# Building an adjacency matrix from edge one-hots on TensorE: source index split into tile and place, one wide moving one-hot per edge tile

## The chip, the cores and the metric

One core of one Trainium2 chip runs the whole program. The metric is the device time of one launch in microseconds (us). The kernel before takes 3161.21 us, the median of 3 runs (3160.83 to 3163.68).

## The reference, cut to what matters

The program is a two-block graph network: 1250 nodes with 768 features, 40,000 edges. Both blocks need the graph only as dense matrices over (source, destination): a count matrix (how many edges go from s to d) and a weighted one (the sum of the weights of these edges, with the identity added).

```python
def _scatter_add(tgt, idx, src, axis=0):
    return tgt.at[idx].add(src)
...
src = jax.random.randint(jax.random.fold_in(_gk, 2), (40000,), 0, 1250, jnp.int32)
dst = jax.random.randint(jax.random.fold_in(_gk, 3), (40000,), 0, 1250, jnp.int32)
_o = jnp.argsort(dst, stable=True)
src = src[_o]
dst = dst[_o]
edge_weight = jax.random.uniform(jax.random.fold_in(_gk, 12), (40000,), jnp.float32, 0.0, 0.999998)
```

The edges are sorted by destination. The change lies wholly in the stage that builds these two matrices, the first of the program; the attention, the mixers and the expert layers that follow it are the same in both kernels.

## The kernel before, in words

**Data.** An edge tile is 128 edges, one per partition; there are 313 of them, held as columns of `src_c`, `dst_c` and the weights. Eight edge tiles (`SPREAD`) form a block, 40 blocks (`NB`) form the stage. As the edges are sorted, the 1024 edges of a block touch a short window of destinations, `WIN` = 38 wide, whose start `base[b]` comes from the data. The weight is split into three bf16 parts (`w_c[0..2]`) that add up to the fp32 value. A slower branch (`Else`) stands for edge lists where the window does not hold; here `flag` is 0 and the first branch runs.

**One block, before.** VectorE (DVE) makes the destination one-hot of all eight tiles in one instruction of 304 (8 x 38) elements (L1645) and its three products with the weight parts, 304 elements each (L1651); that is `destinations`. It sets the window for the next block (L1664, 38 elements, `next_block`), and then makes seven source one-hots of 1250 elements, one per edge tile (L1660, `sources`). The eighth source one-hot is made by ScalarE (ACT) in two passes (L1304, L1306). TensorE (PE) does ten matmuls per edge tile (L890): the stationary operand is a slice of 125 columns of the source one-hot, the moving one is 152 columns (4 kinds x 38) of the destination one-hot; it accumulates over the eight tiles in PSUM, in half of the array `ps` (`par` is the half, block number modulo 2). ACT copies the 1520 columns to SBUF (`stage_block`, L1316 and L1318). GpSimd (POOL) adds them into the big matrices `CT` and `WA` at the window's place (`unstage`): it sums the three weight parts (L749, L752), adds the counts (L750) and the weights (L756), each 125 x 380.

**What orders it.** Each engine runs its instructions in program order; counters (semaphores) join them. `src_hot`, `src_hot_act` and `dst_hot` tell PE that one-hots are there, `tiles_done` tells DVE and ACT that PE is through with a tile and its buffers are free (eight source buffers, `RING`), `staged` and `unstaged` join ACT and POOL. Ahead of the stage DVE runs a chain in which each instruction waits for the one before it (`chain`, L1598 to L1637): the edges are converted, turned and split there. Behind the stage DVE's next work is the first layer norm (L1689 to L1701), and PE's next is the transposes of its output (L931).

```python
            def sources(col, tile0):

                for u in range(SPREAD - 1):
                    dve.wait_ge(ev("tiles_done"), tile0 + (u + 1 - RING + CREDIT))
                    dve.tensor_scalar(oh_src[:, u % RING, :], iota_src, src_c[:, bass.ds(col + u, 1)], None,
                                      ALU.is_equal).then_inc(ev("src_hot"), 1)
```

A scalar operand such as `src_c[:, bass.ds(col + u, 1)]` is called a pointer scalar below: one value per partition, read from SBUF, at an address that a register gives.

Of the kernel before, what the change touches and what calls it, by code (L numbers as in the profile page):

```python
# [46 lines left out]
RING = 8  # L47
# [168 lines left out]
def build(nc: bass.Bass, A, out):  # L216
    packets, pieces, last, packet_at = make_plan()

    with ExitStack() as ctx:
# [61 lines left out]
        def ecut(n):  # L281
# [4 lines left out]
        iota_src = ecut(625).bitcast(FP16)  # L286
        src_c = ecut(ECOLS)
        dst_c = ecut(ECOLS)
        w_c = [ecut(ECOLS // 2).bitcast(BF16) for _ in range(3)]
        w_f = ecut(ECOLS)  # L290
        src_n = ecut(SPREAD * NB)
        far = ecut(NODES // 2).bitcast(FP16)
        viol = ecut(ECOLS)
        iota_0 = ecut(WIN)
        iota_b = ecut(WIN)
# [7 lines left out]
        rawf = ecut(9 * P).rearrange("p (a r e) -> p a r e", a=3, r=3)  # L303
        ecut(2 * NT * KINDS * WIN - 18 * P)
        stage = xt_r[0:TILE, stage0:stage0 + 2 * NT * KINDS * WIN].rearrange("p (b j k w) -> p b j k w", b=2, j=NT, k=KINDS)
        oh_src = h_r[:, 0:RING * 625].bitcast(FP16).rearrange("p (s n) -> p s n", s=RING)
        oh_dst = h_r[:, 5000:5000 + SPREAD * KINDS * WIN].bitcast(BF16)\
            .rearrange("p (b t k w) -> p b t k w", b=2, t=SPREAD, k=KINDS)
# [391 lines left out]
        def _(pool):  # L700
# [10 lines left out]
            own.step(pool.iota(iota_src, [[1, NODES]], base=0, channel_multiplier=0,  # L711
                               allow_small_or_imprecise_dtypes=True))
            own.step(pool.iota(iota_0, [[1, WIN]], base=0, channel_multiplier=0,
# [14 lines left out]
            pool.sem_inc(ev("staged"), 4)  # L728
# [14 lines left out]
            def unstage(b, par, done):  # L743

                at = pool.value_load(basei[0:1, bass.ds(b, 1)], min_val=0, max_val=LAST)
                c = bass.ds(at, WIN)
                pool.wait_ge(ev("staged"), done * 2 + 6)
                k = stage[:, par]
                pool.tensor_tensor(k[:, :, 3, :], k[:, :, 3, :], k[:, :, 2, :], ALU.add).then_inc(ev("unst_b"), 1)  # L749
                pool.tensor_tensor(CT[:, :, c], CT[:, :, c], k[:, :, 0, :], ALU.add).then_inc(ev("unst_a"), 1)  # L750
                pool.wait_ge(ev("unst_b"), done + 1)
                pool.tensor_tensor(k[:, :, 3, :], k[:, :, 3, :], k[:, :, 1, :], ALU.add).then_inc(ev("unst_c"), 1)  # L752
                pool.wait_ge(ev("unst_a"), done + 1)
                pool.wait_ge(ev("unst_c"), done + 1)
                pool.wait_ge(ev("unstaged"), done + 2)
                pool.tensor_tensor(WA[:, :, c], WA[:, :, c], k[:, :, 3, :], ALU.add).then_inc(ev("unstaged"), 1)  # L756
# [87 lines left out]
        def _(pe):  # L844
# [32 lines left out]
            def bank(par, q):  # L877
                return ps[0:TILE, 2 * par + q // 2, 512 * (q % 2):512 * (q % 2) + 512]

            def edge_tiles(par, n, fresh):  # L880

                for u in range(SPREAD):
                    if u < SPREAD - 1:
                        pe.wait_ge(ev("src_hot"), n * (SPREAD - 1) + (u + 1))
                    else:
                        pe.wait_ge(ev("src_hot_act"), n + 1)
                    s = u % RING
                    for j in range(NT):
                        o = KINDS * WIN * (j % 3)
                        mm = pe.matmul(bank(par, j // 3)[:, o:o + KINDS * WIN], oh_src[:, s, j * TILE:j * TILE + TILE],  # L890
                                       oh_dst[:, par, u, :, :], start=(fresh and u == 0 and j % 3 == 0), stop=False,
                                       skip_group_check=True)
                    mm.then_inc(ev("tiles_done"), 1)

            def open_block(par, b):

                pe.wait_ge(ev("staged"), b * 2 + 2)

            def clear(par):
                for q in range(4):  # L900
                    w = KINDS * WIN * (3 if q < 3 else 1)
                    pe.matmul(bank(par, q)[:, 0:w], zero16[:, 0:TILE], zero16[:, 0:w], start=True, stop=False,
                              skip_group_check=True)

            with pe.If(flag == 0):
                with pe.Fori(0, NB // 2) as bp:
                    for par in range(2):
                        b = bp * 2 + par
                        open_block(par, b)
                        pe.wait_ge(ev("dst_hot"), b + 1)  # L910
                        edge_tiles(par, b, True)
            with pe.Else():
                with pe.Fori(0, NB // 2) as bp:
                    for par in range(2):
# [3 lines left out]
                        with pe.Fori(0, CHUNKS) as ch:  # L918
                            n = b * CHUNKS + ch
                            pe.wait_ge(ev("dst_hot"), n + 1)  # L920
                            edge_tiles(par, n, False)
            pe.wait_ge(ev("staged"), 2 * NB + 4)
# [367 lines left out]
        def _(act):  # L1290
# [10 lines left out]
            def source(col, n):  # L1301

                act.wait_ge(ev("tiles_done"), n * SPREAD + CREDIT)
                act.activation(far, iota_src, ACT.Abs, bias=src_n[:, bass.ds(col, 1)]).then_inc(ev("src_far"), 1)  # L1304
                act.wait_ge(ev("src_far"), n + 1)
                act.activation(oh_src[:, RING - 1, :], far, ACT.Relu, bias=onesc, scale=-1.0)\  # L1306
                   .then_inc(ev("src_hot_act"), 1)

            def stage_block(par, b, tiles):
# [3 lines left out]
                src = ps[0:TILE, 2 * par:2 * par + 2, :].rearrange("p s (b n) -> p (s b) n", b=2)  # L1313
                dst = stage[:, par].rearrange("p j k w -> p (j k w)")
                w = KINDS * WIN
                act.activation(dst[:, 0:9 * w].rearrange("p (b n) -> p b n", b=3), src[:, 0:3, 0:3 * w], ACT.Copy)\  # L1316
# [937 lines left out]
```

## Time and profile before

| what | value |
|---|---|
| median of 3 runs | 3161.21 us |
| profiled execution, its own time | 3162.54 us |
| profiled execution, span of its instructions | 3160.8 us |
| PE busy / DVE busy / ACT busy / POOL busy | 2801.1 / 1612.7 / 923.6 / 333.0 us |
| edge stage: first DVE one-hot to the end of the last | 35.2 to 341.9 us |
| PE matmuls of the edge stage (L890) | 3200, 244.2 us busy |
| DVE source one-hots (L1660) | 280, 218.2 us busy |

The span is cut into 40 equal slices of 79 us; the stage fills the first four and part of the fifth. An instruction's duration is longer than the distance to the next one's start where they overlap, so that both are read: durations from the groups, distances from the start times.

### The profile page before, as it was taken

To read this page: it belongs to the slowest core of one execution; us is meant where nothing else is said; L and a number is where in the kernel's file an instruction comes from. 1 tells how busy PE (TensorE), PEld (TensorE's weight loads), DVE (VectorE), ACT (ScalarE), POOL (GpSimd) and SP (SyncE) were. 2 spreads that over 40 slices of the span, in tenths; PEclk is the share of its full clock that TensorE was granted. 3 is DMA by queue.
4 is the path that set the end of the run, shared out by engine and by line. 5 is a ranking of instruction groups with operands and counts; after the bars stand their busy time and mean duration, and the time that the engine had idled before them with its cause. 6 is when DMAs were issued, how large, how long until landed. Compare 5 with 4: busy or idle time off the path is not lost.

```text
span 3160.8 us, 33593 instructions
## 1 busy us (share of the span) xinstructions
PE 2801.1 (89%) x13527; PEld 1971.8 (62%) x13527; DVE 1612.7 (51%) x2217; ACT 923.6 (29%) x974; POOL 333.0 (11%) x314
## 2 busy tenths in 40 slices
PE   4777899999989889699956989996879999899999
PEld 4777565688876556477743855553457777555555
DVE  8999679889973444311133230004267777522220
ACT  3666310077751232111110011011054444321110
POOL 5556230000000011100030000000000000000000
PEclk9999999999999899799976999997989999999999
DMA  9700431121030301477755100000020100200000
GB/s 248 265 0 0 110 94 59 42 71 57 34 64 6 84 7 52 140 250 261 259 150 115 33 17 0 30 30 29 0 80 27 40 27 29 105 10 10 10 10 10
DMA packets 123619, 226.60 MB, mean 72 GB/s; under 512 B 18535, under 2 KB 91788, under 8 KB 123006
## 3 DMA queue, kind: packets, MB, share of 16 engines
q1 hardware_dynamic: 107746, 178.79, 19.0%
q0 software_dynamic: 15760, 46.20, 4.6%
q8 instruction: 84, 1.38, 0.2%
q14 instruction: 29, 0.24, 0.0%
HBM read 158.92 MB, written 66.01 MB: 71 GB/s over the span
## 4 chain that ended last, share of the span: by engine, by line
PE 72%; DVE 18%; issue 3%; DMA 3%; ACT 2%; DVEq 1%; POOL 1%; SPq 0%; ACTq 0%; POOLq 0%
PE ps L939 20%; PE ps L1283 13%; PE ps L1267 13%; DVE arena L1660 5%; PE ps L1163 4%; PE ps L1129 4%; PE ps L956 4%; PE ps L1175 4%; DVE arena L1790 2%; DVE arena L1791 2%; PE ps L1216 1%; DVE small L1689 1%; PE ps L1208 1%; PE ps L1039 1%; DMA arena<-in_x_dram 1%
## 5 line engine op out<-in xcount | busy, mean ns | idle before, releaser
L939 PE MATMUL ps<-arena 128*125 128x384 f32 x2160 | 719.8, 496 | 28.3 <-DVE arena L2124 12.8
L939 PEld LDWEIGHTS ps<-arena 128*125 128x125 f32 x2160 | 412.4, 192 | 324.7 <-issue 34.5
L1283 PE MATMUL ps<-arena 128*125 128x384 f32 x1280 | 414.5, 488 | 14.2 <-DVE arena L2164 14.2
L1267 PE MATMUL ps<-arena 128*128 128x312 f32 (+1 forms) x1536 | 407.2, 428 | 15.2 <-DVE arena L2164 15.2
L1267 PEld LDWEIGHTS ps<-arena 128*128 128x128 f32 x1536 | 292.5, 191 | 129.6 <-issue 16.8
L1283 PEld LDWEIGHTS ps<-arena 128*125 128x125 f32 x1280 | 241.0, 188 | 187.6 <-issue 16.1
L1295 ACT ACTIVATE arena<-ps 128x750 f32<-128x750 f32 (+4 forms) x175 | 133.2, 792 | 722.0 <-PE ps L939 206.3
L890 PE MATMUL ps<-arena 128*125 128x152 bf16 x3200 | 244.2, 234 | 67.2 <-DVE arena L1660 65.6
L2164 DVE SCALAR_TENSOR_TENSOR arena<-arena 128x1250 f32<-128x1250 f32 (+1 forms) x170 | 231.4, 1383 | 114.5 <-PE ps L1267 110.9
L890 PEld LDWEIGHTS ps<-arena 128*125 128x125 f16 x3200 | 222.8, 138 | 88.6 <-DVE arena L1660 87.7
L1727 DVE SCALAR_TENSOR_TENSOR arena<-ps,arena 125x768 f32<-125x768 f32 x30 | 28.7, 956 | 379.1 <-PE ps L1283 291.9
L1660 DVE TENSOR_SCALAR arena<-arena 128x1250 f16<-128x1250 f16 x280 | 218.2, 850 | 0.0
L1039 PE MATMUL ps<-arena 125*125 125x97 f32 x1600 | 182.9, 276 | 5.7 <-DVE arena L1791 5.7
L1039 PEld LDWEIGHTS ps<-arena 125*125 125x125 f32 x1600 | 181.0, 192 | 9.0 <-DVE arena L1791 6.9
L2080 DVE TENSOR_TENSOR arena<-ps,arena 128x768 f32<-128x768 f32 x34 | 32.6, 958 | 271.3 <-PE ps L1175 271.3
L956 PE MATMUL ps<-arena 128*128 128x312 f32 (+7 forms) x544 | 156.6, 449 | 3.2 <-ACT arena L1295 2.2
L1129 PE MATMUL ps<-arena 125*125 125x385 f32 (+1 forms) x400 | 136.4, 497 | 11.3 <-POOL arena L821 11.3
L1783 DVE CUSTOM_DVE_ANT_0 arena<-arena 125x1250 bf16<-125x1250 bf16 x90 | 131.4, 1460 | 23.6 <-DMA arena<-al_src 21.0
L1163 PE MATMUL ps<-arena 128*128 128x256 f32 x612 | 136.8, 383 | 1.1 <-ACT arena L1295 1.1
L1175 PE MATMUL ps<-arena 128*128 128x384 f32 x408 | 134.5, 486 | 0.8 <-ACT arena L1295 0.8
L956 PEld LDWEIGHTS ps<-arena 128*128 128x128 f32 (+3 forms) x544 | 102.7, 191 | 52.1 <-issue 18.2
L1163 PEld LDWEIGHTS ps<-arena 128*128 128x128 f32 x612 | 117.7, 193 | 21.1 <-issue 1.5
(296 smaller groups left out, 2875.2 us busy)
## 6 DMA issues: line engine op xcount, KB each, us to landing
arena<-in_L_ffn_W_dram SPq DMA_DIRECT2D x34, 1152.0 KB, 7.0
xs_rows<-arena SPq DMA_DIRECT2D x1, 30720.0 KB, 99.5
arena<-xs_rows SPq DMA_DIRECT2D x17, 768.0 KB, 7.9
y_rows<-arena POOLq DMA_DIRECT2D x34, 384.0 KB, 3.3
arena<-in_kw_dram SPq DMA_DIRECT2D x24, 512.0 KB, 5.7
arena<-al_dst POOLq DMA_DIRECT2D x18, 625.0 KB, 4.9
arena<-in_kw_dram SPq DMA_DIRECT2D x6, 1536.0 KB, 9.9
arena<-in_x_dram SPq DMA_DIRECT2D x2, 3600.0 KB
```

The source lines that it names most:

```text
L890: mm = pe.matmul(bank(par, j // 3)[:, o:o + KINDS * WIN], oh_src[:, s, j * TILE:j * TILE + TILE], oh_dst[:, par, u, :, :], start=(fresh an ...
L939: mm = pe.matmul(slot(g)[0:TILE, 512 * half:512 * half + HALF], xt[:, k, i * TILE:i * TILE + TILE], w[:, k, :], start=(k == 0), stop=(k == ...
L956: mm = pe.matmul(slot(g)[0:rows, 512 * b:512 * b + w], stat, mov[:, lo + b * w:lo + b * w + w], start=(t == 0), stop=(t == len(terms) - 1))
L1039: mm = pe.matmul(slot(g)[0:TILE, 512 * (j // 5) + 97 * (j % 5):512 * (j // 5) + 97 * (j % 5) + 97], AT[m % AHEAD][:, j * TILE:j * TILE + T ...
L1129: mm = pe.matmul(slot(g)[0:TILE, 512 * b:512 * b + w], AT2[i][:, j * TILE:j * TILE + TILE], H769[:, i, lo:lo + w], start=(i == 0), stop=(i ...
L1163: mm = pe.matmul(slot(g)[:, 0:TAU], w1s[t % 2][:, k, f * P:f * P + P], xsT[t % 2][:, k, :], start=(k == 0), stop=(k == KT - 1))
L1175: mm = pe.matmul(slot(g)[:, 512 * b:512 * b + HALF], hTt[t % 2][:, f, h * P:h * P + P], w2s[t % 2][:, f, b * HALF:b * HALF + HALF], start= ...
L1267: mm = pe.matmul(slot(g)[:, 512 * b:512 * b + wd_], w[:, r % 2, ORDER[p], o * P:o * P + P], feat[place(f)][:, lo + b * wd_:lo + b * wd_ + ...
L1283: mm = pe.matmul(slot(g)[0:TILE, 512 * b:512 * b + HALF], fv[:, q, :], w2c[m][q][:, b * HALF:b * HALF + HALF], start=(p == 0 and q == 0), ...
L1295: give(act.activation(dst, src, func, **kw), g)
L1660: dve.tensor_scalar(oh_src[:, u % RING, :], iota_src, src_c[:, bass.ds(col + u, 1)], None, ALU.is_equal).then_inc(ev("src_hot"), 1)
L2164: return dve.scalar_tensor_tensor(out=out_, in0=in_, scalar=edge, in1=of, op0=op, op1=ALU.mult)
```

## The change

The source index is split in two: its tile, `group` (0 to 9), and its place in the tile, `member` (0 to 124). One moving one-hot of 380 elements (`SPOTS` = 10 tiles x 38) carries tile and destination together: it is 1 at 38 x group + offset in the window. Four stationary one-hots of 125 elements carry the place: plain, and times each of the three weight parts (with a second ALU operation and a second pointer scalar). PE then does four matmuls of 380 columns per edge tile in place of ten of 152; the three weight parts accumulate in the same PSUM bank, so that POOL has two additions per block in place of four and ACT copies 760 columns in place of 1520. All one-hots are now made by DVE, five instructions per edge tile, 40 per block; there is a buffer for each of the 16 tiles of two blocks. ACT makes none. The chain ahead of the stage computes `group`, `member` and `spot_of` for all edges at once. The weight parts are kept in fp32 (`w_p`).

On DVE, ahead of the stage and in its first block, the rows before (L1645 and L1651 are the destination one-hot and its products, L1660 the source one-hots; an ISA row is a register instruction of the queue that forms an address):

```order
L1608 CAST arena<-arena 128x384
L1609 TENSOR_TENSOR arena<-arena 128x384
L1610 CAST arena<-arena 128x384
L1611 TENSOR_TENSOR arena<-arena 128x384
L1612 CAST arena<-arena 128x384
L1620 TENSOR_SCALAR arena<-ps 128x40
```

and now:

```order
L1583 MEMSET arena 128x384
L1587 CAST arena<-arena 128x384
L1588 CAST arena<-arena 128x384
L1590 TENSOR_TENSOR arena<-arena 128x384
L1587 CAST arena<-arena 128x384
L1588 CAST arena<-arena 128x384
L1590 TENSOR_TENSOR arena<-arena 128x384
L1587 CAST arena<-arena 128x384
L1588 CAST arena<-arena 128x384
L1592 SCALAR_TENSOR_TENSOR arena<-arena 128x384 x9
L1594 SCALAR_TENSOR_TENSOR arena<-arena 128x384
L1603 TENSOR_SCALAR arena<-ps 128x40
```

The chain between the edges' arrival and the window's start has grown from five instructions to nineteen. In the loop, DVE before, the start of a block:

```order
L1645 TENSOR_TENSOR arena<-arena 128x8x38
L1651 ISA
L1651 TENSOR_TENSOR arena<-arena 128x8x38
L1651 ISA
L1651 TENSOR_TENSOR arena<-arena 128x8x38
L1651 ISA
L1651 TENSOR_TENSOR arena<-arena 128x8x38
L1664 ISA
L1664 TENSOR_SCALAR arena<-arena 128x38
L1659 REGISTER_ALU
L1660 ISA
L1660 TENSOR_SCALAR arena<-arena 128x1250
```

and now, one edge tile and the start of the next:

```order
L1629 ISA
L1629 TENSOR_SCALAR arena<-arena 128x380
L1631 ISA
L1631 TENSOR_SCALAR arena<-arena 128x125
L1633 ISA
L1633 TENSOR_SCALAR arena<-arena 128x125
L1633 ISA
L1633 TENSOR_SCALAR arena<-arena 128x125
L1633 ISA
L1633 TENSOR_SCALAR arena<-arena 128x125
L1628 REGISTER_ALU
L1629 ISA
```

Eleven wide and one narrow instruction per block have become forty narrow ones, each with a register instruction ahead of it. On PE each group of ten matmuls is one of four (L885), with one wait ahead of it as before:

```order
L883 ISA
L885 MATMUL ps<-arena 125x380 x4
L883 REGISTER_ALU
L885 MATMUL ps<-arena 125x380 x4
L883 REGISTER_ALU
L885 MATMUL ps<-arena 125x380 x4
```

The diff, without the arena's layout, the unused branch and the parts that only follow from these:

```diff
@@ POOL: per block
-                pool.wait_ge(ev("staged"), done * 2 + 6)
+                pool.wait_ge(ev("staged"), done + 3)
                 k = stage[:, par]
-                pool.tensor_tensor(k[:, :, 3, :], k[:, :, 3, :], k[:, :, 2, :], ALU.add).then_inc(ev("unst_b"), 1)
-                pool.tensor_tensor(CT[:, :, c], CT[:, :, c], k[:, :, 0, :], ALU.add).then_inc(ev("unst_a"), 1)
-                pool.wait_ge(ev("unst_b"), done + 1)
-                pool.tensor_tensor(k[:, :, 3, :], k[:, :, 3, :], k[:, :, 1, :], ALU.add).then_inc(ev("unst_c"), 1)
+                pool.tensor_tensor(CT[:, :, c], CT[:, :, c], k[:, 0], ALU.add).then_inc(ev("unst_a"), 1)
                 pool.wait_ge(ev("unst_a"), done + 1)
-                pool.wait_ge(ev("unst_c"), done + 1)
                 pool.wait_ge(ev("unstaged"), done + 2)
-                pool.tensor_tensor(WA[:, :, c], WA[:, :, c], k[:, :, 3, :], ALU.add).then_inc(ev("unstaged"), 1)
+                pool.tensor_tensor(WA[:, :, c], WA[:, :, c], k[:, 1], ALU.add).then_inc(ev("unstaged"), 1)
@@ PE: per edge tile
-                    if u < SPREAD - 1:
-                        pe.wait_ge(ev("src_hot"), n * (SPREAD - 1) + (u + 1))
-                    else:
-                        pe.wait_ge(ev("src_hot_act"), n + 1)
-                    s = u % RING
-                    for j in range(NT):
-                        o = KINDS * WIN * (j % 3)
-                        mm = pe.matmul(bank(par, j // 3)[:, o:o + KINDS * WIN], oh_src[:, s, j * TILE:j * TILE + TILE],
-                                       oh_dst[:, par, u, :, :], start=(fresh and u == 0 and j % 3 == 0), stop=False,
-                                       skip_group_check=True)
+                    pe.wait_ge(ev("hot"), n * SPREAD + (u + 1))
+                    for k in range(KINDS):
+                        mm = pe.matmul(bank(par, min(k, 1)), oh_src[:, par, u, k, :], oh_spot[:, par, u, :],
+                                       start=(fresh and u == 0 and k < 2), stop=False, skip_group_check=True)
                     mm.then_inc(ev("tiles_done"), 1)
@@ ACT: per block; both passes of source() are gone
-                act.activation(dst[:, 0:9 * w].rearrange("p (b n) -> p b n", b=3), src[:, 0:3, 0:3 * w], ACT.Copy)\
+                act.activation(stage[:, par].rearrange("p k j w -> p k (j w)"), banks_of(par), ACT.Copy)\
                    .then_inc(ev("staged"), 1)
-                act.activation(dst[:, 9 * w:10 * w], src[:, 3, 0:w], ACT.Copy).then_inc(ev("staged"), 1)
@@ DVE: ahead of the stage
-            own.step(dve.tensor_scalar(src_n, ps[:, 0, 0:NB * SPREAD], -1.0, None, ALU.mult))
+            own.step(dve.memset(group, 0.0))
             own.settle()
-            chain(dve.tensor_copy(w_c[0], w_f))
-            chain(dve.tensor_tensor(w_f, w_f, w_c[0], ALU.subtract))
-            chain(dve.tensor_copy(w_c[1], w_f))
-            chain(dve.tensor_tensor(w_f, w_f, w_c[1], ALU.subtract))
-            chain(dve.tensor_copy(w_c[2], w_f))
+            for k in range(3):
+                chain(dve.tensor_copy(w_16, w_f))
+                chain(dve.tensor_copy(w_p[k], w_16))
+                if k < 2:
+                    chain(dve.tensor_tensor(w_f, w_f, w_p[k], ALU.subtract))
+            for t in range(1, NT):
+                chain(dve.scalar_tensor_tensor(out=group, in0=src_c, scalar=float(t * TILE), in1=group,
+                                               op0=ALU.is_ge, op1=ALU.add))
+            chain(dve.scalar_tensor_tensor(out=member, in0=group, scalar=-float(TILE), in1=src_c,
+                                           op0=ALU.mult, op1=ALU.add))
@@
-            dve.tensor_scalar(iota_b, iota_0, base[:, 0:1], None, ALU.add).then_inc(ev("next_block"), 1)
+            chain(dve.scalar_tensor_tensor(out=grouped(spot_of), in0=grouped(group), scalar=float(WIN), in1=grouped(offset),
+                                           op0=ALU.mult, op1=ALU.add))
@@ DVE: per block; destinations(), sources() and next_block() are replaced
+            def one_hots(par, col, tile0, ring, spot):
+
+                for u in range(SPREAD):
+                    dve.wait_ge(ev("tiles_done"), tile0 + (u + 1 - ring + CREDIT))
+                    dve.tensor_scalar(oh_spot[:, par, u, :], spots, spot(u), None, ALU.is_equal)
+                    at = member[:, bass.ds(col + u, 1)]
+                    dve.tensor_scalar(oh_src[:, par, u, 0, :], within, at, None, ALU.is_equal)
+                    for k in range(3):
+                        ins = dve.tensor_scalar(oh_src[:, par, u, 1 + k, :], within, at, w_p[k][:, bass.ds(col + u, 1)],
+                                                ALU.is_equal, ALU.mult)
+                    ins.then_inc(ev("hot"), 1)
...
-                        destinations(par, b * SPREAD, b, b * SPREAD - SPREAD + CREDIT, b)
-                        next_block(b)
-                        sources(b * SPREAD, b * SPREAD)
+                        one_hots(par, b * SPREAD, b * SPREAD, 2 * SPREAD, lambda u: spot_of[:, bass.ds(b * SPREAD + u, 1)])
```

`spots` and `within` are fp16 index rows (0 to 379, 0 to 124), the one-hots are bf16, the pointer scalars fp32.

## Rows read from the trace of the kernel before

**Rows 1.** The page: busy time of each engine; PE's granted clock in 40 slices.

```profile
PE 2801.1 (89%) x13527; PEld 1971.8 (62%) x13527; DVE 1612.7 (51%) x2217; ACT 923.6 (29%) x974; POOL 333.0 (11%) x314
...
PEclk9999999999999899799976999997989999999999
```

**Rows 2.** Busy time by stretch: the steady part of the edge stage.

```profile
core 0: us, PE busy (x) PEld busy (x) DVE busy (x) ACT busy (x) POOL busy (x), PEclk, DMA share, GB/s
...
73.30:341.90 268.60, 210.70 (x2776) 190.51 (x2777) 263.74 (x418) 165.29 (x157) 162.36 (x140) 1.00 0.25 85
```

**Rows 3.** Groups in 73.3 to 341.9 us: count, busy us, mean ns, idle before.

```profile
L890 PE MATMUL ps<-arena 128*125 128x152 bf16 x2776 | 210.9, 232 | 58.5 <-DVE arena L1660 57.4
L1660 DVE TENSOR_SCALAR arena<-arena 128x1250 f16<-128x1250 f16 x245 | 193.8, 861 | 0.0
```

**Rows 4.** DVE in order of time, its first block (start, us, instruction, count).

```profile
35.19 0.48 DVE L1645 TENSOR_TENSOR arena<-arena 128x304 bf16<-128x304 f32 x1 [1.45 <-issue]
...
36.97 0.24 DVE L1664 TENSOR_SCALAR arena<-arena 128x38 f32<-128x38 f32 x1
37.12 3.27 DVE L1660 TENSOR_SCALAR arena<-arena 128x1250 f16<-128x1250 f16 x7
40.31 0.47 DVE L1645 TENSOR_TENSOR arena<-arena 128x304 bf16<-128x304 f32 x1
```

**Rows 5.** POOL in order of time in a steady block, beside L1660 on DVE.

```profile
206.76 1.18 POOL L750 TENSOR_TENSOR arena<-arena 125x380 f32 x1
207.89 1.24 POOL L752 TENSOR_TENSOR arena<-arena 125x380 f32<-125x380 f32 x1
```

**Rows 6.** DVE in order of time, 2194 to 2200.5 us.

```profile
2194.97 5.13 DVE L2124 TENSOR_SCALAR arena<-arena,small 128x1250 f32<-128x1250 f32 x6 [4.51 <-ACT arena L1295]
```

**Rows 7.** All engines in order of time behind the stage: POOL alone, DVE's layer norm.

```profile
346.12 0.87 POOL L750 TENSOR_TENSOR arena<-arena 125x380 f32 x1
346.95 0.99 POOL L752 TENSOR_TENSOR arena<-arena 125x380 f32<-125x380 f32 x1
...
351.12 0.86 DVE L1692 BATCH_NORM_AGGREGATE small<-small 125x2 f32<-125x12 f32 x10
...
352.72 5.99 DVE L1701 TENSOR_SCALAR arena<-arena,small 125x768 f32<-125x768 f32 x10
```

**Rows 8.** DVE in order of time ahead of the stage.

```profile
26.10 0.48 DVE L1605 TENSOR_SCALAR arena<-ps 128x320 f32<-128x320 f32 x1
26.62 0.36 DVE L1608 CAST arena<-arena 128x384 bf16<-128x384 f32 x1
27.01 0.56 DVE L1609 TENSOR_TENSOR arena<-arena 128x384 f32<-128x384 f32 x1
27.61 0.36 DVE L1610 CAST arena<-arena 128x384 bf16<-128x384 f32 x1
...
28.99 0.20 DVE L1620 TENSOR_SCALAR arena<-ps 128x40 f32<-128x40 f32 x1
```

**Rows 9.** The chain of waits around 204 us; DVEq is DVE's instruction queue.

```profile
203.34 0.06 DVEq L1651
...
203.47 0.06 DVEq L1664
...
203.69 0.06 DVEq L1660
...
203.91 0.06 DVEq L1660
```

**Rows 10.** PE in order of time, in the stage.

```profile
71.20 1.53 PE L890 MATMUL ps<-arena 128*125 128x152 bf16 x20 [0.33 <-DVE arena L1660]
```

**Rows 11.** Busy time by stretch, L931 only in each; PEclk is PE's clock.

```profile
353.50:356.20 2.70, 2.66 (x13) 2.69 (x14) 2.70 (x5) 0.80 (x1) 0.00 (x0) 0.50 0.00 0
356.60:359.20 2.60, 2.60 (x27) 2.60 (x25) 2.10 (x4) 2.60 (x5) 0.00 (x0) 1.00 0.00 0
```

**Rows 12.** All engines in order of time, the first 22 us.

```profile
2.96 1.18 POOL L711 IOTA arena<- 128x1250 f16 x1
...
7.13 14.80 DVE L1598 CAST arena<-arena 128x384 f32<-128x384 int32 x2 [7.13 <-DMA arena<-in_edge_weight_dram]
```

More of the change, by code:

```diff
@@ L284, in ecut @@
             return xt_r[:, eo[0] - n:eo[0]]
-        iota_src = ecut(625).bitcast(FP16)
+        spots = ecut(SPOTS // 2).bitcast(FP16)
+        within = ecut(64).bitcast(FP16)[:, 0:TILE]
         src_c = ecut(ECOLS)
         dst_c = ecut(ECOLS)
-        w_c = [ecut(ECOLS // 2).bitcast(BF16) for _ in range(3)]
+        w_p = [ecut(ECOLS) for _ in range(3)]
         w_f = ecut(ECOLS)
-        src_n = ecut(SPREAD * NB)
-        far = ecut(NODES // 2).bitcast(FP16)
+        w_16 = ecut(ECOLS // 2).bitcast(BF16)
+        group = ecut(ECOLS)
+        member = ecut(ECOLS)
+        offset = ecut(ECOLS)
         viol = ecut(ECOLS)
-        iota_0 = ecut(WIN)
-        iota_b = ecut(WIN)
+        spot_of = ecut(ECOLS)
+        spot8 = ecut(2 * SPREAD).rearrange("p (b t) -> p b t", b=2)
+        out8 = ecut(SPREAD)
+        off8 = ecut(SPREAD)
         zero16 = ecut(256).bitcast(BF16)
@@ new lines, in keys @@
+            def keys(par, col, b, n):
+                own8 = ev("keys")
+                dve.tensor_scalar(off8, dst_c[:, bass.ds(col, SPREAD)], base[:, bass.ds(b, 1)], None, ALU.subtract)\
+                   .then_inc(own8, 1)
+                dve.wait_ge(own8, n * 5 + 1)
+                dve.tensor_scalar(out8, off8, 0.0, None, ALU.is_lt).then_inc(own8, 1)
+                dve.wait_ge(own8, n * 5 + 2)
+                dve.scalar_tensor_tensor(out=out8, in0=off8, scalar=float(WIN), in1=out8, op0=ALU.is_ge, op1=ALU.add)\
+                   .then_inc(own8, 1)
+                dve.scalar_tensor_tensor(out=off8, in0=group[:, bass.ds(col, SPREAD)], scalar=float(WIN), in1=off8,
+                                         op0=ALU.mult, op1=ALU.add).then_inc(own8, 1)
+                dve.wait_ge(own8, n * 5 + 4)
+                dve.scalar_tensor_tensor(out=spot8[:, par, :], in0=out8, scalar=-4096.0, in1=off8, op0=ALU.mult, op1=ALU.add)\
+                   .then_inc(own8, 1)
+                dve.wait_ge(own8, n * 5 + 5)
@@ L1743, in _ @@
             dve.wait_ge(ev("x"), 32)
-            layer_norm("xn", acc, H, free=(ev("staged"), 2 * NB + 4))
+            layer_norm("xn", acc, H, free=(ev("staged"), NB + 2))
             exps = [0]
```

80 lines of the change are left out of this document (22 added, 58 removed).

## The prediction

> **What bounds the kernel now.** I read the page first. PE is busy 2801 us of the span and DVE 1613 [rows 1], but that is an average over stages, and the change touches only the stage from 35.2 to 341.9 us, 306.7 us long. The busy times by stretch say who limits it: from 73.3 to 341.9 us DVE is busy 263.7 of 268.6 us, PE 210.7, ACT 165.3, POOL 162.4 [rows 2]. The groups say the same from the other side: PE's matmuls L890 sat idle 58.5 us, 57.4 of them for L1660, while L1660 has no idle time ahead of it [rows 3]. So the edge stage lasts as long as DVE's instructions, and what the change does to PE, ACT or POOL counts only as far as it reaches DVE.
>
> It reaches DVE at one point. DVE's first block runs from 35.19 to 40.31, 5.12 us [rows 4]; POOL has nothing to add yet. All 40 blocks take 306.7, so those after the first two take (306.7 - 2 x 5.12) / 38 = 7.80 us, 2.68 us more. The durations show where it goes: seven L1660 take 3.27 us in the first block, so the distance between two starts is (3.27 - 0.54) / 6 = 0.455 us (a single one lasts 0.54) [rows 4], but the mean duration later is 0.861 us [rows 3]. There POOL's additions start 1.13 us apart [rows 5], though with DVE elsewhere they are 0.83 us apart [rows 7]. Both engines stretch, each by about the other's work. DVE loses 2.68 / 4 = 0.67 us per POOL addition. The start-up shows the same in large: two casts at 7.13 us took 14.80 us beside POOL's long memsets [rows 12].
>
> **What a DVE instruction costs.** The new stage is made of short ones, so I need fixed cost and slope. Two pointer scalars, fp32: 1250 elements start (5.13 - 0.93) / 5 = 0.84 us apart (one lasts about 0.93) [rows 6], 768 elements (5.99 - 0.67) / 9 = 0.59 [rows 7]. Slope 0.25 / 482 = 0.52 ns per element, fixed part 0.59 - 0.40 = 0.19 us. One pointer scalar, fp32: L1664, 38 elements, is followed after 0.15 us [rows 4]; less 0.02 that is 0.13 fixed. L1660, 16-bit, one pointer scalar: 0.455 - 0.13 = 0.325 for 1250 elements, 0.26 ns each. That is one fixed cost at 38 and at 1250 elements, so I carry it to the widths between.
>
> **The change, part by part.**
> - *Per edge tile on DVE.* The moving one-hot of 380, one pointer scalar: 0.13 + 0.10 = 0.23 us. The plain stationary one of 125: 0.13 + 0.03 = 0.16. Three with a weight and so two pointer scalars: 3 x (0.19 + 0.03) = 0.67. Sum 1.06 us; a block 8.48, where it was 5.12. The elements fell from 1250 to 880 per tile; the instructions rose from 12 to 40 per block, and at these widths the fixed part is most of each.
> - *DVE's queue.* Register instructions start 0.13 us apart, and 0.22 where a wait's register operation lies between [rows 9]. Five per tile: 0.22 + 4 x 0.13 = 0.74 us. Below 1.06, hidden behind the engine; it decides only if the engine should be quicker.
> - *POOL's additions:* two per block in place of four. Each held DVE up 0.67 us; the new ones are as wide. 2 x 0.67 = 1.35 us per block, in 38 blocks 51 us. Bounds: 0, if DVE's short instructions slip between, and 1.8, if each addition's own length (0.87 and about 0.99) is lost in full. I take 1.35: an addition is as long as it was, and DVE's fixed part runs on under it as before.
> - *The stage:* 40 x 8.48 = 339, plus 51, is 390 us in place of 306.7: **+83.5 us**.
> - *Ahead of the stage* each instruction waits for the last. Removed: 0.52 (L1605), L1608 to L1612 from 26.62 to 28.99, 2.37, and 0.15 for L1636 (as L1664): 3.0 us [rows 8, 4]. Added: six casts at 0.39, two subtractions and eleven two-operand instructions (nine for group, member, spot_of) at 0.60, a memset between 0.1 and 0.5: 2.3 + 7.8 + 0.4 = 10.5. Net +7.5. POOL's index row of 1250 (1.18 us [rows 12]) is one of 380 and one of 125: its memsets, and with them the casts that they hold, come about 0.7 us sooner. **+6.8 us.**
> - *PE.* 20 matmuls of 152 columns take 1.53 us, so one is 0.067 at most [rows 10]; 380 columns, 2.5 times as many, are 0.165. Four: 0.66 us per tile, where the ten take 0.65. PE waits for DVE as before, with 16 tiles of buffers. No time gained or lost.
> - *ACT* loses both one-hot passes and half its copy. It ended nobody's wait before; nothing. Its two-pass one-hot did carry an eighth of the source one-hots, though, and that work is DVE's now (it is in the 1.06).
> - *Behind the stage* DVE's layer norm follows its last one-hot at once, and PE waits for it. POOL ends its last block sooner, with two additions fewer, but layer norm needs neither. All that follows moves by the sum.
>
> The sum: 83.5 + 6.8 = **+90.3 us**. On the profiled execution's own 3162.5 us that makes 3252.8; the median of the runs lies 1.3 lower, so I say **3251 us**.
>
> **Rules of the Trainium skill.** POOL's additions start 0.3 us further apart beside L1660 than alone [rows 5, 7], and L1660 lasts 0.86 us on average where it lasts 0.54 alone [rows 3, 4]. The Trainium skill, SBUF — State Buffer, on the two sides and their contention, says that the pair of ports which DVE and GpSimd share is an exclusive lock held for a whole instruction, so that the later one blocks; the trace agrees (1.13 against 0.83 us for POOL). By it DVE can lose up to the addition's whole length, 1.8 us per block, and the sum would be 18 us higher. On the fixed cost the two differ. The Trainium skill, VectorE: DVE Perf Modes, section on the fixed extra latency, tabulates 58 cycles plus elements over the mode's factor at 0.96 GHz, and adds that a longer fixed term was measured; the same section advises tiles of 512 elements or more, which speaks against this change. By its table 380 and 125 elements would cost 0.16 and 0.09 us as an estimate, a tile 0.53. Rows 4 and 7 have 0.13 and 0.19 fixed, and I go by them.
>
> **The rivals.**
> - *Short instructions are cheap (faster).* If the fixed part were 0.07 us, whatever the pointers, a tile would cost 0.10 + 4 x 0.03 + 5 x 0.07 = 0.57 us, and DVE's queue would set the pace with 0.74. For it: ten aggregates of 12 elements take 0.86 us, so they start (0.86 - 0.16) / 9 = 0.08 us apart [rows 7]. Against it: they have no pointer scalar, and L1664 has one, is as short, and takes 0.15. The time: 40 x 8 x 0.74 = 237 plus half of the port waits, 26, is 263: -44 + 7 = 3124 us. It decides from the point where the stage is under 300 us, a block under 7.5, a tile under (7.5 - 1.35) / 8 = 0.77 us, that is 0.06 less per instruction than I have. The table of the Trainium skill's page above is this rival's case.
> - *The second pointer is free on short instructions.* Then three of five cost 0.16: 960 x 0.06 = 58 us less, 3193 us. The two rows with 0.19 are wide fp32 ones; no row shows a short one with two pointers.
> - *The odd width.* 125 is odd, and every 16-bit row that I have is even. At one element where L1660 takes four, 125 elements cost 0.13 and not 0.03: +0.10 x 4 x 320 = 125 us, 3376 us. At half the rate +42, 3293 us.
> - *PE's clock.* PE's share of the stage falls from 78% [rows 2] to 0.66 / 1.22, 54%. Where its clock stands at 0.50 the chip ran 13 transposes in 2.7 us, at 1.00 it ran 27 in 2.6 [rows 11], at 1.2 and 2.4 GHz. At the low level all the way a tile is 0.66 x 2 = 1.3 us on PE, and PE would bind with 40 x 8 x 1.3 = 416 us: 3277 us. Against it: the clock stood at 1.00 through the steady stage, in which PE rested a fifth of the time [rows 2], and DVE leaves it less work per us only, no longer rest than a few tenths.
> - *It does not do what it says:* PE still could be shown to bind; rows 3 exclude it.
>
> **How the numbers follow.** My forecast gets 0.62, the free second pointer 0.12, the odd width 0.09 (half of it at half rate), PE's clock 0.08, cheap short instructions 0.09. The range, 3190 to 3300 us, holds the forecast with both bounds of the port waits (-51 and +18), the free pointer, the half rate and the clock; outside are the faster rival and the full odd width. A change under 0.2%, 6 us, cannot be told from none. Faster 0.08, same 0.02, slower 0.90.
>
> **What would show it.** Right: L1629 and L1631 followed after 0.23 and 0.16 us, L1633 after 0.22 where POOL rests; the first block about 8.5 us and the later ones 9.8; DVE 97% busy from about 42 to 432 us, PE waiting for L1633; all after it unchanged. Wrong: idle time on DVE ahead of the one-hots (PE or the queue binds), a block under 7.5 us, or a first block of 10 us and more (odd width).

## The result, and the profile after

The changed kernel takes 3253.1 us, the median of 4 runs (3250.78 to 3259.32), against 3162.28 us for the kernel before (4 runs, 3160.83 to 3163.68). The ratio is 1.0293, 95% interval 1.0279 to 1.0306: 90.8 us slower. The forecast was 3251 us. The profiled execution took 3252.26 us, its instructions span 3250.5.

The page of the kernel after, its busy times and PE's granted clock, against [rows 1]:

```profile
PE 2863.0 (88%) x11607; PEld 1939.9 (60%) x11607; DVE 1715.3 (53%) x3350; ACT 791.7 (24%) x854; POOL 229.2 (7%) x234
...
PEclk9888889999999999979996798998989999999999
```

DVE has 103 us more to do and PE's clock shows eights in the slices of the edge stage, where it had nines. The busy times by stretch, against [rows 2] (the columns are PE, PEld, DVE, ACT, POOL with their counts, then the granted clock):

```profile
41.90:50.60 8.70, 6.97 (x28) 4.38 (x28) 8.58 (x40) 1.05 (x1) 0.00 (x0) 1.00 1.04 371
...
73.30:435.30 362.00, 276.96 (x1172) 170.81 (x1171) 362.00 (x1469) 52.01 (x54) 74.89 (x74) 0.85 0.18 63
```

In the steady part DVE is busy 362.0 of 362.0 us. The groups of the same part, against [rows 3], columns as there:

```profile
L885 PE MATMUL ps<-arena 128*125 128x380 bf16 x1172 | 277.6, 386 | 85.0 <-DVE arena L1633 84.1
L1633 DVE TENSOR_SCALAR arena<-arena 128x125 bf16<-128x125 f16 x882 | 247.6, 334 | 0.0
...
L1631 DVE TENSOR_SCALAR arena<-arena 128x125 bf16<-128x125 f16 x294 | 94.7, 322 | 0.0
L1629 DVE TENSOR_SCALAR arena<-arena 128x380 bf16<-128x380 f16 x293 | 90.0, 307 | 0.0
L753 POOL TENSOR_TENSOR arena<-arena 125x380 f32 x37 | 41.3, 1116 | 279.5 <-ACT arena L1295 279.5
L756 POOL TENSOR_TENSOR arena<-arena 125x380 f32 x37 | 34.2, 924 | 9.6 <-POOL arena L753 9.6
```

PE idled 85.0 us, 84.1 of them for L1633, so DVE sets the stage's length as before. DVE in order of time, the first edge tiles and the start of the chain of nine comparisons ahead of them, against [rows 4] and [rows 8]:

```profile
29.52 5.30 DVE L1592 SCALAR_TENSOR_TENSOR arena<-arena 128x384 f32<-128x384 f32 x9
34.86 0.56 DVE L1594 SCALAR_TENSOR_TENSOR arena<-arena 128x384 f32<-128x384 f32 x1
...
41.95 0.32 DVE L1629 TENSOR_SCALAR arena<-arena 128x380 bf16<-128x380 f16 x1 [1.37 <-issue]
42.19 0.25 DVE L1631 TENSOR_SCALAR arena<-arena 128x125 bf16<-128x125 f16 x1
42.35 0.75 DVE L1633 TENSOR_SCALAR arena<-arena 128x125 bf16<-128x125 f16 x3
43.17 0.32 DVE L1629 TENSOR_SCALAR arena<-arena 128x380 bf16<-128x380 f16 x1
...
44.24 0.32 DVE L1629 TENSOR_SCALAR arena<-arena 128x380 bf16<-128x380 f16 x1
44.47 0.26 DVE L1631 TENSOR_SCALAR arena<-arena 128x125 bf16<-128x125 f16 x1
44.63 0.76 DVE L1633 TENSOR_SCALAR arena<-arena 128x125 bf16<-128x125 f16 x3
45.30 0.32 DVE L1629 TENSOR_SCALAR arena<-arena 128x380 bf16<-128x380 f16 x1
```

The second tile starts at 43.17 and the third at 44.24, the fourth at 45.30: 1.07 and 1.06 us per tile. From a start to the next: 0.23 us for the one-hot of 380 (44.24 to 44.47), 0.16 for the plain one of 125 (44.47 to 44.63), and (45.30 - 44.63) / 3 = 0.223 for each weighted one. The first block lasts 8.65 us and the later ones 9.86 on average. What lies between is again beside POOL, against [rows 5], all engines in order of time:

```profile
200.66 1.19 POOL L753 TENSOR_TENSOR arena<-arena 125x380 f32 x1 [7.50 <-ACT arena L1295]
200.78 0.30 DVE L1629 TENSOR_SCALAR arena<-arena 128x380 bf16<-128x380 f16 x1
...
201.01 0.90 DVE L1631 TENSOR_SCALAR arena<-arena 128x125 bf16<-128x125 f16 x1
201.82 1.48 DVE L1633 TENSOR_SCALAR arena<-arena 128x125 bf16<-128x125 f16 x3
202.11 0.92 POOL L756 TENSOR_TENSOR arena<-arena 125x380 f32 x1 [0.26 <-POOL arena L753]
```

L753 starts at 200.66; L1631, 0.25 us long in the first block, now lasts 0.90, and the three L1633 behind it take 1.48 in place of 0.75 because L756 starts in their midst.

Where the 89.7 us between the two spans (3160.8 and 3250.5) lie, by start times of DVE's first one-hot and first layer-norm instruction:

| stretch | before | after | difference |
|---|---|---|---|
| to the first one-hot | 35.19 | 41.95 | +6.8 |
| edge stage | 306.6 | 393.4 | +86.8 |
| all behind it | 2819.0 | 2815.2 | -3.8 |

### The profile page after: what moved, and what is told of

The parts are those of the page before. It is cut to its first block, busy times and chain, and to the rows that moved or that the text cites. A ratio compares the mean times of both kernels' runs of the same rounds, so it can differ in the third digit from the quotient of the medians.

```text
span 3250.5 us, 31666 instructions
## 1 busy us (share of the span) xinstructions
PE 2863.0 (88%) x11607; PEld 1939.9 (60%) x11607; DVE 1715.3 (53%) x3350; ACT 791.7 (24%) x854; POOL 229.2 (7%) x234
## 4 chain that ended last, share of the span: by engine, by line
PE 73%; DVE 16%; issue 5%; DMA 3%; ACT 2%; DVEq 1%; POOL 1%; SPq 0%; POOLq 0%; ACTq 0%
PE ps L929 21%; PE ps L1273 13%; PE ps L1257 13%; PE ps L1153 4%; PE ps L1119 4%; PE ps L1165 4%; PE ps L946 4%; DVE arena L1633 3%; PE ps L885 3%; DVE arena L1775 2%; DVE arena L1776 2%; PE ps L1206 1%; DVE arena L1629 1%; DVE small L1674 1%; DVE arena L1631 1%
## 5 line engine op out<-in xcount | busy, mean ns | idle before, releaser
L885 PE MATMUL ps<-arena 128*125 128x380 bf16 x1280 | 303.2, 386 | 94.8 <-DVE arena L1633 93.8
L885 PEld LDWEIGHTS ps<-arena 128*125 128x125 bf16 x1280 | 187.0, 161 | 210.8 <-DVE arena L1633 168.1
L1633 DVE TENSOR_SCALAR arena<-arena 128x125 bf16<-128x125 f16 x960 | 267.7, 332 | 0.0
```

Of the source, the lines that this page charges most:

```text
L885: mm = pe.matmul(bank(par, min(k, 1)), oh_src[:, par, u, k, :], oh_spot[:, par, u, :], start=(fresh and u == 0 and k < 2), stop=False, ski ...
L1633: ins = dve.tensor_scalar(oh_src[:, par, u, 1 + k, :], within, at, w_p[k][:, bass.ds(col + u, 1)], ALU.is_equal, ALU.mult)
```

## The experiments

The theory is the prediction's: DVE's time in the stage is the sum of a fixed cost per instruction (0.13 us with one pointer scalar, 0.19 with two, so 0.06 per pointer scalar on 0.07), a little per element, and a wait at each of POOL's additions, called the port wait here. The rivals are the width (125 elements at a poor rate, so that elements cost and not instructions) and PE (its clock is down at 0.85).

### POOL's additions cut short, in both kernels

```diff
-            own.step(pool.memset(ct_r[0:TILE, 0:6400], 0.0))
+            own.step(pool.memset(CT, 1.0))
...
-                pool.tensor_tensor(CT[:, :, c], CT[:, :, c], k[:, 0], ALU.add).then_inc(ev("unst_a"), 1)
+                pool.tensor_tensor(CT[:, 0:1, c], CT[:, 0:1, c], k[:, 0, 0:1], ALU.add).then_inc(ev("unst_a"), 1)
...
-                pool.tensor_tensor(WA[:, :, c], WA[:, :, c], k[:, 1], ALU.add).then_inc(ev("unstaged"), 1)
+                pool.tensor_tensor(WA[:, 0:1, c], WA[:, 0:1, c], k[:, 1, 0:1], ALU.add).then_inc(ev("unstaged"), 1)
```

> The changed kernel with POOL's two additions per block cut from 125 x 380 to 125 x 38 elements (only the first source tile is added; nine tenths of both matrices are left out, and the count matrix starts as ones so that no later sum is empty). Theory, DVE's instructions and the port that POOL holds: the later blocks fall from 9.87 to about 8.6 us, those of the first block, 39 blocks x 2 additions x about 0.6 us, so about 3253 - 48 = 3205 us. Rival, PE sets the pace (its clock stands at 0.85 in the stage and it idles only for want of work): blocks stay at 9.9 us and the time at 3253.

Measured: 3209.6 us (2 runs), 43.5 less than the changed kernel. The groups say how (100 to 300 us, columns as above), and a steady block took 8.59 us in place of 9.87:

```profile
L885 PE MATMUL ps<-arena 128*125 128x380 bf16 x746 | 160.0, 337 | 40.2 <-DVE arena L1633 40.2
L1633 DVE TENSOR_SCALAR arena<-arena 128x125 bf16<-128x125 f16 x560 | 142.0, 310 | 0.0
...
L1631 DVE TENSOR_SCALAR arena<-arena 128x125 bf16<-128x125 f16 x186 | 47.5, 255 | 0.0
```

L1631 is back from a mean of 322 to 255 ns. Over 39 blocks 1.28 us each are 49.8; 5.7 us were lost ahead of the stage, where the memset of ones took 10.76 us in place of 5.43 and held DVE's casts. PE has the same matmuls at a mean of 337 ns in place of 386, with its clock at 1.00, so this run alone could not tell a faster PE from a freed DVE. The trace of the changed kernel can: DVE was busy 362.0 of 362.0 us there and never waited for PE, and the block here is DVE's own 8.49 us and 0.1 more. The rival on PE falls.

> The kernel before with its four additions per block cut in the same way. Theory: DVE loses 2.68 us per block to them, so the blocks fall from 7.8 to about 5.2 us and the time to about 3162 - 98 = 3064 us. PE has 5.2 us of matmuls per block and may then bind at 5.3. Rival, the long L1660 are slow for another reason than POOL (ACT reading beside them, for one): blocks stay near 7.8 us and the time near 3162.

Measured: 3089.5 us (2 runs), ratio 0.9777 (0.9758 to 0.9797) to the kernel before; 3064 was expected. The group of L1660 (100 to 250 us):

```profile
L1660 DVE TENSOR_SCALAR arena<-arena 128x1250 f16<-128x1250 f16 x182 | 87.0, 547 | 0.0
```

Its mean fell to 547 ns from 861, so the port waits of DVE are gone as the theory has it, but the stage fell by 73.6 us and not by 98 (and it starts 5.4 us later, behind the longer memset of ones). Its blocks are 5.27 and 6.48 us by turns. The waits between engines, 100 to 250 us (who waited for whom: us, times, longest):

```profile
DVE arena L1645 <- PE ps L890: 14.4, 12, 1.2
...
PE ps L890 <- ACT arena L1306: 12.0, 12, 1.0
```

and ACT in order of time:

```profile
199.30 1.28 ACT L1304 ACT_TABLE_LOAD   x1
...
200.59 1.34 ACT L1304 ACTIVATE arena<-arena 128x1250 f16<-128x1250 f16 x1
...
201.96 1.34 ACT L1306 ACTIVATE arena<-arena,small 128x1250 f16<-128x1250 f16 x1
...
204.26 1.31 ACT L1316 ACTIVATE arena<-ps 125x1368 f32<-125x1368 f32 x1 [0.96 <-PE ps L890]
```

ACT makes the eighth source one-hot in two passes of 1.34 us, and in every second block it loads a table first, 1.28 us. With POOL out of the way PE waits 1.0 us for it, and DVE for PE. In the kernel before this was hidden: there PE waited for L1660 only [rows 3].

### The pointer scalar and the weight

```diff
-                        ins = dve.tensor_scalar(oh_src[:, par, u, 1 + k, :], within, at, w_p[k][:, bass.ds(col + u, 1)],
-                                                ALU.is_equal, ALU.mult)
+                        ins = dve.tensor_scalar(oh_src[:, par, u, 1 + k, :], within, at, None, ALU.is_equal)
```

> The changed kernel with the three weighted one-hots made without the weight, so with one pointer scalar and one operation in place of two; the weights are left out, widths and counts stay. Theory, fixed cost per instruction and per pointer: 960 instructions become 0.06 us shorter each, 58 us in all, 3195 us; a block 8.4 us. Rival, the width (125 elements at a poor rate) is what costs: nothing changes, 3253 us.

Measured: 3197.1 us (2 runs), 56.0 less. A block took 8.44 us. DVE in order of time, its first tile:

```profile
42.20 0.26 DVE L1631 TENSOR_SCALAR arena<-arena 128x125 bf16<-128x125 f16 x1
42.36 0.58 DVE L1633 TENSOR_SCALAR arena<-arena 128x125 bf16<-128x125 f16 x3
42.85 0.32 DVE L1629 TENSOR_SCALAR arena<-arena 128x380 bf16<-128x380 f16 x1
```

(42.85 - 42.36) / 3 = 0.163 us, the same as the plain one-hot (42.20 to 42.36), where it was 0.223. Width and count have stayed. So the second pointer with its operation costs 0.06 us on an instruction of 125 elements as on the wide ones of [rows 6, 7], and 125, odd as it is, costs 0.03 us of elements beside 0.13 fixed. This run took both away, the pointer and the operation; that the pointer is what costs is suggested by the run e8_quick_group_alone below, where an instruction of 384 elements with two operations and no pointer (L1591) lasts 0.36 us, as the cast of 384 in [rows 8] does with no operation at all. The rival on the odd width falls, and so does the free second pointer.

### Fewer instructions, the same elements

```diff
-                    for k in range(3):
-                        ins = dve.tensor_scalar(oh_src[:, par, u, 1 + k, :], within, at, w_p[k][:, bass.ds(col + u, 1)],
-                                                ALU.is_equal, ALU.mult)
-                    ins.then_inc(ev("hot"), 1)
+                    if u % q == q - 1:
+                        lo = u + 1 - q
+                        dve.wait_ge(ev("plain"), tile0 + (u + 1))
+                        dve.tensor_tensor(oh_src[:, par, lo:lo + q, 1:4, :],
+                                          oh_src[:, par, lo:lo + q, 0:1, :].broadcast_to([P, q, 3, TILE]),
+                                          w_all[:, bass.ds(col + lo, q), :].unsqueeze(3).broadcast_to([P, q, 3, TILE]),
+                                          ALU.mult).then_inc(ev("hot"), q)
```

The plain one-hot now counts in `plain`, for which the product waits.

> The changed kernel with its weighted one-hots made by one tensor-by-tensor product for four edge tiles (1500 elements), two per block in place of 24 instructions. Same elements, same matmuls, same POOL and ACT work; all of the output is computed. Theory, cost by count: 8 x 0.23 + 8 x 0.16 + 2 x (0.07 + 1500 x 1.04 ns) = 6.4 us, plus 1.4 us of port waits, 7.8 us per block in place of 9.87: about 3253 - 83 = 3170 us, though the products run at a quarter of the element rate. Rival, elements cost and not instructions: 3000 elements per block at 1.04 ns in place of 0.26 make it 2.3 us per block slower, 3345 us. Rival, PE's clock: PE gets its tiles in bursts of four, is colder, and the time stays or rises.

Measured: 3186.3 us (4 runs), ratio 1.0082 (1.0066 to 1.0099) to the kernel before, 67 us less than the changed one. DVE in order of time:

```profile
44.24 0.26 DVE L1633 TENSOR_SCALAR arena<-arena 128x125 bf16<-128x125 f16 x1
44.66 1.72 DVE L1637 TENSOR_TENSOR arena<-arena 128x1500 bf16<-128x1500 bf16 x1 [0.16 <-DVE arena L1633]
46.29 0.32 DVE L1631 TENSOR_SCALAR arena<-arena 128x380 bf16<-128x380 f16 x1
```

One product takes 1.63 us (44.66 to 46.29), as forecast, and stands for twelve instructions of 0.223, 2.68 us, though each of its elements costs four times as much. The direction and the size are the theory's; the miss of 16 us comes from a term that I left out. The product waits until the last plain one-hot has landed: 0.42 us from that one's start to its own and not 0.16, twice per block, 21 us in all. Undisturbed blocks are 6.92 us where 6.4 was expected, and port waits of 1.3 bring the mean to 8.18. The granted clock was 0.92 between 100 and 250 us, where the changed kernel has 0.85, so PE was not colder for getting its tiles in bursts, and again the blocks did not wait for PE.

### The weighted one-hots moved to ACT

```diff
+            def weighted(par, b, us):
+                for u in us:
+                    act.wait_ge(ev("plain"), b * SPREAD + (u + 1))
+                    for k in (1, 2):
+                        ins = act.activation(oh_src[:, par, u, 1 + k, :], oh_src[:, par, u, 0, :], ACT.Copy,
+                                             scale=w_p[k][:, bass.ds(b * SPREAD + u, 1)])
+                    ins.then_inc(ev("hot_act"), 1)
...
+                        weighted(par, b, range(2))
+                        stage_block(1 - par, b - 1, SPREAD)
+                        weighted(par, b, range(2, SPREAD))
```

ACT makes two tiles of a block before it copies the block ahead out of PSUM, so that it does not wait for PE there. DVE makes the plain one-hot of a tile first, ahead of the wide one, and PE waits for both engines.

> The changed kernel with two of the three weighted one-hots made by ACT, as the plain one-hot times a pointer scalar (16 instructions of 125 elements per block); DVE has three instructions per edge tile. Theory, DVE's instruction count: 0.23 + 0.16 + 0.22 = 0.61 us per tile, 4.9 per block, plus 1.4 us of port waits, 6.3 us per block in place of 9.87; ACT needs 16 x about 0.27 + 0.82 = 5.1, PE 5.3. About 3253 - 141 = 3112 us. Rival, PE's clock or PE's waits on two engines set the pace: the blocks stay over 8 us, 3180 us or more.

Measured: 3101.2 us (4 runs), ratio 0.9815 (0.9799 to 0.9832) to the kernel before: faster than both, and 11 us less than expected. Blocks of 6.09 us where 6.3 was expected: DVE's own part is the 4.9 of the forecast (4.91 in the second block, which POOL leaves alone), the port waits are 1.2 and not 1.4. Busy by stretch, columns as above:

```profile
60.00:280.00 220.00, 202.68 (x1170) 146.24 (x1168) 220.00 (x864) 201.65 (x622) 74.64 (x73) 1.00 0.36 126
```

DVE is still full, 220.0 of 220.0; PE and ACT are nearly so, and the clock is at 1.00.

> As the run with two, but ACT makes all three weighted one-hots (24 instructions per block), DVE two instructions per tile. Theory: DVE 8 x 0.39 = 3.1 plus 1.4, 4.5 us per block; ACT 24 x about 0.27 + 0.82 = 7.3 binds in its place, so 7.3 us per block and 3253 - 101 = 3152 us, slower than with two. Rival, ACT's short instructions cost 0.2 us or less: ACT 5.6, PE 5.3 to 6 bind, 3095 us, faster than with two.

Measured: 3158.2 us (10 runs), ratio 0.9995 (0.9985 to 1.0004). ACT binds:

```profile
60.00:330.00 270.00, 233.90 (x1130) 130.86 (x1130) 153.44 (x565) 270.00 (x886) 64.81 (x72) 1.00 0.29 102
```

and its instructions in order of time:

```profile
199.73 4.51 ACT L1307 ACTIVATE arena<-arena 128x125 bf16<-128x125 bf16 x15
204.07 0.86 ACT L1297 ACTIVATE arena<-ps 125x760 f32<-125x760 f32 x1
204.75 5.68 ACT L1307 ACTIVATE arena<-arena 128x125 bf16<-128x125 bf16 x19
```

(4.51 - 0.39) / 14 = 0.29 us from start to start (one of them lasts 0.39), and 0.68 for the copy: 24 x 0.29 + 0.68 = 7.6 us, the block's measured 7.63; 7.3 was expected, with 0.27 per instruction. The third of the three costs more on ACT than it frees on DVE.

### The chain ahead of the stage

```diff
-            for t in range(1, NT):
-                chain(dve.scalar_tensor_tensor(out=group, in0=src_c, scalar=float(t * TILE), in1=group,
-                                               op0=ALU.is_ge, op1=ALU.add))
+            chain(dve.tensor_scalar(group, src_c, 1.0 / TILE, 0.5 / TILE - 0.5, ALU.mult, ALU.add))
+            chain(dve.tensor_scalar(group, group, 12582912.0, -12582912.0, ALU.add, ALU.add))
```

> As the run with two weighted one-hots on ACT, and the source tile found by two instructions (scale and shift, then rounding by adding and subtracting a large constant) in place of the nine comparisons ahead of the stage, 5.3 us. Theory, the chain ahead of the stage lies on the path in full: the first one-hot starts 4.6 us sooner and the time is 4.6 us less than with two, 3107 us. Rival, the start is set by something else (POOL's memsets, PE): no difference.

> The changed kernel with only the nine comparisons ahead of the stage replaced by two instructions. The nine take 5.3 us, the two take 2 x 0.33 + waits, 0.8. Theory, that chain lies on the path in full: the first one-hot starts at 37.4 in place of 41.95 us and the time is 4.6 us less, 3248.5 us. Rival, something else sets the start: 3253 us.

In the changed kernel alone: 3246.0 us (5 runs, 3244.8 to 3251.9), 7.1 less by the medians. DVE in order of time:

```profile
29.53 0.36 DVE L1591 TENSOR_SCALAR arena<-arena 128x384 f32<-128x384 f32 x1
29.92 0.36 DVE L1592 TENSOR_SCALAR arena<-arena 128x384 f32<-128x384 f32 x1
30.32 0.56 DVE L1593 SCALAR_TENSOR_TENSOR arena<-arena 128x384 f32<-128x384 f32 x1
...
37.41 0.32 DVE L1628 TENSOR_SCALAR arena<-arena 128x380 bf16<-128x380 f16 x1 [1.36 <-issue]
```

The first one-hot starts at 37.41 in place of 41.95, 4.5 us sooner, and the stage has its old length (393.1 us). On top of the ACT version the medians differ by 1.5 us only, 3099.7 (3094.4 to 3103.3) against 3101.2 where 4.6 was expected, while the profiled execution reaches the layer norm 4.8 us sooner (280.34 against 285.15). The start of the stage moves as the theory says in both; by the run times alone neither comparison is sharp, since what lies behind the stage varies by as much.

### One more one-hot on ACT

```diff
-                    for k in (1, 2):
+                    for k in ((0, 1, 2) if u == 4 else (1, 2)):
```

> Two weighted one-hots per edge tile on ACT and the quick source tile, as before, and in one edge tile of eight ACT makes the third too. In that run the blocks took 6.09 us, DVE's 4.91 and 1.2 of port waits; ACT's instructions start 0.29 us apart, so it needed 16 x 0.29 + 0.68 = 5.3. Theory: DVE 6.09 - 0.22 = 5.87, ACT 5.6, PE 5.3, so 0.22 x 40 = 9 us less than the 3100 us of the run with the quick source tile: 3091 us. Rival, PE is at its limit already (it waits for two engines by turns): 3100 us.

Measured: 3094.3 us (5 runs, 3091.8 to 3096.3), ratio 0.9790 (0.9777 to 0.9803) to the kernel before, the fastest here. Half of the expected gain came: the stage took 239.0 us where it was 242.9. The second block, the last that POOL leaves alone, is 4.69 us where the ACT version without this had 4.91, as expected. But the later blocks did not fall by 0.22 us each. To the nineteenth they vary, many at the forecast's 5.87 and some up to 6.69, 5.99 on average, and 3.8 of the 4.0 us are gained there; from the twentieth on they are 6.08, where the version without this has 6.09. POOL in order of time, in the one part and in the other:

```profile
122.70 1.15 POOL L753 TENSOR_TENSOR arena<-arena 125x380 f32 x1 [3.49 <-ACT arena L1297]
...
128.47 0.89 POOL L753 TENSOR_TENSOR arena<-arena 125x380 f32 x1 [3.39 <-ACT arena L1297]
...
134.23 0.95 POOL L753 TENSOR_TENSOR arena<-arena 125x380 f32 x1 [3.70 <-ACT arena L1297]
...
140.00 1.04 POOL L753 TENSOR_TENSOR arena<-arena 125x380 f32 x1 [3.60 <-ACT arena L1297]
```
```profile
242.44 1.14 POOL L753 TENSOR_TENSOR arena<-arena 125x380 f32 x1 [3.75 <-ACT arena L1297]
...
248.52 1.14 POOL L753 TENSOR_TENSOR arena<-arena 125x380 f32 x1 [3.74 <-ACT arena L1297]
```

In the first part the first additions start 5.77 us apart, less than DVE's 5.99 per block, and their length goes round (1.15, 0.89, 0.95, 1.04): they meet other instructions of DVE each time. In the second part they start 6.08 us apart, as DVE's blocks do, and each lasts 1.14, so the meeting is always the same one, and DVE loses 6.08 - 4.69 = 1.4 us per block in place of 1.2. The trace shows what changes between the two: between 47 and 155 us ACT never waits for a plain one-hot (L1648), from 160 us on it does so in every block, about 0.25 us. ACT, which started behind, has caught up with DVE by then. Why the fixed meeting takes back just what DVE was spared was not tried and stays open.

## Why the prediction was right

The bound was DVE, before and after, and the sum came out within 1 us. By its own steps:

| step | predicted | measured |
|---|---|---|
| a tile on DVE | 1.06 us | 1.06 to 1.07 |
| fixed cost with one, with two pointers | 0.13, 0.19 | 0.13, 0.19 (0.163 and 0.223 with 125 elements) |
| port wait per addition | 0.67 | (9.87 - 8.49) / 2 = 0.69, 8.49 being eight undisturbed tiles of 1.06 |
| ahead of the stage | +6.8 us | +6.8 |
| the stage | +83.5 us | +86.8 |
| behind it | 0 | -3.8 |
| sum | +90.3 us | +89.7 in the traces, +90.8 by the medians |

*Fixed cost and slope.* This step carried the result. Rows at 38, 768 and 1250 elements gave it, and it held at 125 and 380. The run with one pointer shows the 0.06 us of the second with its operation, the run with batched products shows that the count of instructions is what costs. The Trainium skill, VectorE: DVE Perf Modes, section on the fixed extra latency, has a table by which 125 elements would take 0.09 us as an estimate; the trace has 0.16 and 0.22, and the measurement decides. The same section of the Trainium skill has a row for ScalarE (224 cycles and one per element, at 1.2 GHz), which makes an estimate of 0.29 us for 125 elements, and there the trace agrees (0.29).

*The port.* It was worked out by subtraction from a first block that POOL left alone. The two runs with short additions show it directly: 1.28 us per block after, and L1660 back at 547 ns before. The loss per addition is nearly the same in both kernels (0.67 and 0.69), so half as many additions give back half of it, 1.3 us per block, against 3.4 us that the instructions add. The step holds as to what POOL's additions cost DVE; what the two engines share was not taken apart by a run.

*Small misses of the stage, 3.3 us.* The first block took 8.65 and not 8.48: its first tile took 1.22 us, with a pause ahead of the second tile whose cause stays open (in e8_quick_group_alone, with the same loop, it is missing and the first block takes 8.49); only one block is undisturbed and not two, since POOL adds the first while DVE makes the second, 1.4 us; the rest is the hundredths per block.

*PE.* The step that PE gains and loses nothing held, but the reason against the clock rival did not: I wrote that DVE leaves PE no longer rest than a few tenths and took the clock at 1.00. It was 0.85 in the steady stage, at the low level (1.2 GHz) part of the time, with PE waiting 84.1 us for L1633. PE in order of time:

```profile
135.38 5.10 PE L885 MATMUL ps<-arena 128*125 128x380 bf16 x20 [0.20 <-DVE arena L1633]
...
144.21 0.86 PE L885 MATMUL ps<-arena 128*125 128x380 bf16 x4 [1.61 <-DVE arena L1633]
```

The rests reach 1.6 us, once in a block, where POOL's additions hold DVE up. The low level cost nothing: the matmuls then start 0.32 us apart where they start 0.16 apart at the high one, so four take 1.3 us, more than DVE's 1.06; but such a stretch has both levels, its twenty matmuls take 5.10 us, 1.02 per tile, and 16 buffers carry PE over it. In the run with short additions the clock was at 1.00 and the blocks were DVE's sum all the same.

*Behind the stage.* The 3.8 us there offset the miss in the stage, which is luck. The code is the same; in the nine experiments this part took 2812.2 to 2822.5 us, whatever stood ahead of it.

## What to carry to other kernels

Count instructions before elements: at 125 to 380 elements of 16 bits the fixed part, 0.13 us with one pointer scalar and 0.19 with two, is more than what the elements cost (0.03 to 0.10), and the rewrite that cut the elements per edge tile from 1250 to 880 made the stage 28% longer by raising instructions from 12 to 40 per block. Look for a stretch in which the suspected neighbour is silent, the first block here, and take the undisturbed price from it: that separated DVE's own work from the waits for POOL. What a change frees elsewhere is worth something only when work is moved onto it: ACT and POOL were freed, and only when ACT got two of three one-hots did the new layout beat the old one, by 2%. And a cut on the engine that binds need not arrive: the last 0.22 us per block taken from DVE shortened the early blocks only.

## What the runs showed of the hardware that I had not expected

- ACT loads a table in every second block, 1.28 us each, in both kernels. It is not the mixing of functions that does it: in the changed kernel and in e1_short_adds the loop on ACT has only copies, and they still have it (e1_short_adds, groups of 100 to 300 us, beside 24 copies):

```profile
L1295 ACT ACT_TABLE_LOAD x12 | 15.4, 1283 | 0.2
```

  In the runs with one-hots on ACT, which begin them ahead of the loop, no load stands in the loop. What decides it was not tried. In the kernel before, the load and the two passes of the source one-hot became what PE waited for in every second block as soon as POOL's additions were short.
- PE's granted clock fell to 0.85 with 277.6 us of matmuls in 362 us (77% busy, where 78% went with 1.00 before); between groups of four matmuls it rested, 1.6 us at the longest. With blocks of 8.59 us in place of 9.87 the clock stood at 1.00. The kernel before kept 1.00 too, with rests of up to 1.4 us, so which difference brought the clock down is not shown.
- The four stationary one-hots of a tile lie 250 bytes apart, so every second one starts off a 4-byte boundary, and their width is odd; they ran at the rate of the wide, even ones all the same: 0.163 us with one pointer, of which 0.13 are fixed.
- A tensor-by-tensor product on DVE that lasts 1.7 us makes POOL wait as POOL makes DVE wait: L754, 0.87 us alone, took 1.73 on average in the run with batched products, and 0.94 to 0.96 in those steady blocks where it met no product.
